# First cross-attention: one unit in four turned by TensorE, two score buffers, jobs moved off VectorE

## What is computed

```python
q = (x @ Wq + bq).reshape(1, B * N, H, hd);  kv = (cond @ Wkv + bkv)...
q = _fq_sym(q * scale, axis=-1); k = _fq_sym(k, axis=-1); v = _fq_sym(v, axis=2)
attn = softmax(einsum('bhqd,bhkd->bhqk', q, k), axis=-1)
attn = _fq_unsigned(attn, axis=-1)          # 0..255 steps of the row's largest value
out = einsum('bhqk,bhkd->bhqd', attn, v)
x = layernorm(x + out @ Wp + bp)
```

## Time and profile before

| | us |
|---|---|
| median of three runs (3065.53 to 3074.6) | 3072.57 |
| profiled execution | 3072.58 |
| its span, first to last instruction | 3070.2 |
| the attention part, first to last pass of VectorE (985.18 to 1683.08) | 697.9 |

### The profile page before, as it was taken

One profiled execution on the slowest core, in us unless ns is written; L12 is line 12 of the kernel. 1 busy time (PEld: TensorE's weight loads), 2 busy tenths in 40 slices (PEclk: granted clock), 3 DMA queues, 4 the chain that ended last, 5 costly groups with the idle time before them and its releaser, 6 DMA issues. The chain is left out here.

```text
span 3070.2 us, 48513 instructions
## 1 busy us (share of the span) xinstructions
PE 2597.4 (85%) x16300; PEld 1616.7 (53%) x16470; DVE 1887.5 (61%) x3971; ACT 1498.4 (49%) x2696; POOL 449.3 (15%) x679
## 2 busy tenths in 40 slices
PE   4999999999975677767776797899868789999997
PEld 2777777777753233333333454555445545555554
DVE  5677777677757899999998112566546622323232
ACT  1555555555544688888887111566545511111110
POOL 1111111112110121222221000111122200000000
PEclk9999999999997788888877898999989989999999
DMA  4000000000001999999999000000022000000000
GB/s 178 1 1 0 0 0 0 0 0 0 0 25 34 198 198 196 198 195 197 197 198 198 24 0 23 1 0 0 0 72 76 18 1 1 0 0 0 0 0 27
DMA packets 566849, 173.12 MB, mean 56 GB/s; under 512 B 535445, under 2 KB 564945, under 8 KB 565713
## 3 DMA queue, kind: packets, MB, share of 16 engines
q1 hardware_dynamic: 562168, 163.91, 28.5%
q10 hardware_dynamic: 4568, 7.74, 0.7%
HBM read 35.29 MB, written 2.10 MB: 12 GB/s over the span
## 5 line engine op out<-in xcount | busy, mean ns | idle before, releaser
L1577 DVE TENSOR_SCALAR_CACHE_REDUCE x_row<-x_p_s,x_nsq 128x1024 f32<-128x1024 f32 x512 | 622.9, 1276 | 15.3 <-PE x_p_s L1395 15.3
L1457 ACT ACTIVATE x_ints<-x_row,x_nb 128x2048 uint16<-128x2048 f32 x256 | 511.6, 1999 | 111.2 <-DMA x_turned<-x_ints 70.2
L1395 PE MATMUL x_p_s<-x_kT,x_qz 128*128 128x512 bf16 x937 | 346.0, 457 | 163.9 <-DVE x_row L1577 151.4
L2384 DVE TENSOR_TENSOR f_h<-f_act_g,f_p_u 128x512 f32<-128x512 f32 (+1 forms) x132 | 90.7, 687 | 521.1 <-PE f_p_y L2277 451.3
L2327 ACT ACTIVATE f_act_g<-f_p_g 128x512 f32<-128x512 f32 (+1 forms) x132 | 78.4, 597 | 548.1 <-PE f_p_g L2262 548.1
L2262 PE MATMUL f_p_g<-f_xT,f_wg 128*128 128x512 f32 (+1 forms) x528 | 258.4, 613 | 16.8 <-ACT f_xT L2314 10.1
L2262 PE MATMUL f_p_u<-f_xT,f_wu 128*128 128x512 f32 (+1 forms) x528 | 252.4, 601 | 0.0
L2277 PE MATMUL f_p_y<-f_wd,f_h 128*128 128x256 f32 (+1 forms) x1056 | 247.5, 379 | 0.0
L2277 PEld LDWEIGHTS f_p_y<-f_wd,f_h 128*128 128x128 f32 (+1 forms) x1056 | 200.6, 190 | 77.2 <-issue 55.6
L1395 PEld LDWEIGHTS x_p_s<-x_kT,x_qz 128*128 128x128 bf16 x1024 | 72.5, 104 | 316.1 <-DVE x_row L1577 293.4
L1408 PEld LDWEIGHTS x_p_o<-x_vi,x_turned 128*128 128x128 f16 x4096 | 144.2, 100 | 144.4 <-DMA x_turned<-x_ints 80.1
(11 more groups left out here) (357 smaller groups left out, 4804.0 us busy)
## 6 DMA issues: line engine op xcount, KB each, us to landing
x_turned<-x_ints SPq DMA_TRANSPOSE x256, 4.8
f_wg<-in_L_ffn_w_dram SPq DMA_DIRECT2D x2, 1408.0 KB, 7.3
f_wu<-in_L_ffn_w_dram SPq DMA_DIRECT2D x2, 1408.0 KB, 7.1
f_wd<-in_L_ffn_w_dram SPq DMA_DIRECT2D x1, 2816.0 KB, 11.1
a_wq<-in_L_attn_Wq_dram SPq DMA_DIRECT2D x1, 2048.0 KB, 8.2
a_wk<-in_L_attn_Wlk_dram SPq DMA_DIRECT2D x1, 2048.0 KB, 17.4
a_wv<-in_L_attn_Wlv_dram ACTq DMA_DIRECT2D x1, 2048.0 KB, 17.9
a_wo<-in_L_attn_Wo_dram ACTq DMA_DIRECT2D x1, 2048.0 KB, 23.6
```

What stands on the lines that cost most here:

```text
L1395: mm = pe.matmul(p_s[n % SLOTS][:, c * BANK:(c + 1) * BANK], qz[b % 2][:, par, a, :], kT[:, a, at:at + BANK], start=True, stop=True)
L1457: act.activation(ints[k][:, :], rows[k][:, :, :].rearrange("p s n -> p (s n)"), ACT.Exp, bias=nb[:, k:k + 1], scale=-1.0, accum_out=esum[: ...
L1577: dve.tensor_scalar(rows[k][:, half, :], p_s[n % SLOTS][:, :], nsq[:, b % 2, h:h + 1], HIGHEST, ALU.mult, ALU.min, accum_out=(low if half ...
L2384: i = dve.tensor_tensor(h[n % 2][0:m, :], act_g[n % 2][0:m, :], p_u[n % 2][0:m, :], ALU.mult)
```

## The change

One unit in four (u % 4 = 3, BY_ARRAY) is no longer transposed by a DMA. TensorE transposes its 16 blocks of 128 x 128 with the identity into a new PSUM tile `p_t` (two banks), three units after the scores, behind that unit's values. ScalarE copies `p_t` to `turned` as 1024 32-bit integers, after the next unit's exponential. To make room, `p_s` has two buffers instead of three. The residual is added in PSUM by a matmul of the identity with x within `project_o`, ScalarE copies the sum to y (`result_up`), and `residual` leaves VectorE. `scale`, the negated scale and `variance` go to GpSimd. The jobs move by one or two units: `turn_reps` to 9, `turn_o` to 12, `project_o` to 14, ScalarE's copies to 7, 8, 10 and 13, `inverse` to j=5, `statistics` and `moments` to 15, GpSimd's last three to 15.

```diff
     HIGHEST = 3.0e38
-    ROWS_KEPT, SLOTS, LATE = 4, 3, 6
+    ROWS_KEPT, SLOTS, LATE = 4, 2, 6
+    BY_ARRAY = ROWS_KEPT - 1
     PER_TILE = 2 * PAIRS
...
         p_s = [ps(f"p_s{i}", [P, HALF]) for i in range(SLOTS)]
+        p_t = ps("p_t", [P, 4 * BANK], BF16)
         p_o, p_w = ps("p_o", [P, BANK]), ps("p_w", [P, BANK])
         s_made, half_up, nb_up, e_up, o_made = (sem(n) for n in ("s_made", "half_up", "nb_up", "e_up", "o_made"))
-        t_in = [sem(f"t_in{k}") for k in range(ROWS_KEPT)]
+        t_in = [sem(f"t_in{k}") for k in range(BY_ARRAY)]
+        t_made, t_read = sem("t_made"), sem("t_read")
         x_turned, xT_up, q_made, q_up, amax_up, scl_up, rec_up, nsq_up = (sem(n) for n in (
...
                 k = u % ROWS_KEPT
-                sp.wait_ge(e_up, u + 1)
-                after(sp, o_made, u - ROWS_KEPT + 1)
-                sp.dma_start(turned[k][:, :, :], ints[k][:, :], transpose=True).then_inc(t_in[k], 16)
+                if k != BY_ARRAY:
+                    sp.wait_ge(e_up, u + 1)
+                    after(sp, o_made, u - ROWS_KEPT + 1)
+                    sp.dma_start(turned[k][:, :, :], ints[k][:, :], transpose=True).then_inc(t_in[k], 16)
                 if u == PER_TILE:
...
                 pe.matmul(p_w[:, 0:H], core.ones[:, :], core.bias("L0_xattn_bp"), start=True, stop=False)
+                pe.matmul(p_w[:, 0:H], core.ident[:, :], core.x[:, b, :], start=False, stop=False)
                 for t in range(KT):
...
                     mm.then_inc(s_made, 1)
+            def turn(u):
+                pe.wait_ge(e_up, u + 1)
+                after(pe, t_read, u // ROWS_KEPT)
+                for c in range(B):
+                    mm = pe.transpose(p_t[:, c * P:(c + 1) * P], ints[BY_ARRAY][:, c * P:(c + 1) * P].bitcast(BF16), core.identb[:, :])
+                mm.then_inc(t_made, 1)
+
             def values(u):
...
                     after(pe, o_read, b)
-                pe.wait_ge(t_in[k], 16 * (u // ROWS_KEPT + 1))
+                if k == BY_ARRAY:
+                    pe.wait_ge(t_read, u // ROWS_KEPT + 1)
+                else:
+                    pe.wait_ge(t_in[k], 16 * (u // ROWS_KEPT + 1))
                 for c in range(B):
...
                     values(u - LATE)
-                jobs(u, {1: [(turn_x, 1)], 3: [(project_q, 1)], 8: [(turn_reps, 1)], 11: [(turn_o, -1)], 13: [(project_o, -1)]})
+                if 0 <= u - 3 < UNITS and (u - 3) % ROWS_KEPT == BY_ARRAY:
+                    turn(u - 3)
+                jobs(u, {1: [(turn_x, 1)], 3: [(project_q, 1)], 9: [(turn_reps, 1)], 12: [(turn_o, -1)], 14: [(project_o, -1)]})
         @block.scalar
...
                 act.copy(oT[:, :, :].rearrange("p t n -> p (t n)"), p_w[:, 0:H]).then_inc(oT_up, 1)
+            def result_up(b):
+                act.wait_ge(y_made, b + 1)
+                after(act, x_up, b)
+                act.copy(y[:, :], p_w[:, 0:H]).then_inc(y_up, 1)
+
             def exps(u):
...
                 act.wait_ge(nb_up, u + 1)
-                after(act, t_in[k], 16 * (u // ROWS_KEPT))
+                if k == BY_ARRAY:
+                    after(act, t_made, u // ROWS_KEPT)
+                else:
+                    after(act, t_in[k], 16 * (u // ROWS_KEPT))
                 act.activation(ints[k][:, :], rows[k][:, :, :].rearrange("p s n -> p (s n)"), ACT.Exp, bias=nb[:, k:k + 1], scale=-1.0,
                                accum_out=esum[:, b, h:h + 1]).then_inc(e_up, 1)
+
+            def take_turned(u):
+                act.wait_ge(t_made, u // ROWS_KEPT + 1)
+                after(act, o_made, u - ROWS_KEPT + 1)
+                act.copy(turned[BY_ARRAY][:, :, :].rearrange("p k n -> p (k n)").bitcast(I32), p_t[:, :].bitcast(I32)).then_inc(t_read, 1)
             x_turned_up(0)
...
                     exps(u)
-                jobs(u, {1: [(query_up, 1)], 6: [(reps_up(0), 1)], 7: [(reps_up(1), 1)], 9: [(o_turned_up, -1)]})
+                if 0 <= u - 1 < UNITS and (u - 1) % ROWS_KEPT == BY_ARRAY:
+                    take_turned(u - 1)
+                jobs(u, {1: [(query_up, 1)], 7: [(reps_up(0), 1)], 8: [(reps_up(1), 1)], 10: [(o_turned_up, -1)], 13: [(result_up, -1)]})
         @block.gpsimd
...
                 return ap.rearrange("p (h d) -> p h d", d=XD)
+            def scales(b):
+                pool.wait_ge(amax_up, b + 1)
+                after(pool, rec_up, b)
+                pool.tensor_scalar(scl[:, :], amax[:, :], 1.0 / QMAX, FLOOR, ALU.mult, ALU.max).then_inc(scl_up, 1)
+
+            def negated(b):
+                pool.wait_ge(scl_up, b + 1)
+                after(pool, half_up, 2 * PER_TILE * (b - 1))
+                pool.tensor_scalar(nsq[:, b % 2, :], scl[:, :], -1.0, None, ALU.mult).then_inc(nsq_up, 1)
+
             def integers(b):
...
                 pool.tensor_tensor(o[:, :], o_raw[:, :], svu[:, :], ALU.mult).then_inc(o_up, 1)
+            def variance(b):
+                pool.wait_ge(mean_up, b + 1)
+                pool.tensor_scalar(mv[:, 1:2], mv[:, 1:2], LN_EPS, None, ALU.add).then_inc(var_up, 1)
+
             def root(b):
...
                 pool.tensor_scalar(core.x[:, b, :], y[:, :], mv[:, 0:1], ln_r[:, 0:1], ALU.subtract, ALU.mult).then_inc(x_up, 1)
-            for piece in (integers, whole, copies):
+            for piece in (scales, negated, integers, whole, copies):
                 piece(0)
...
                     shift(u)
-                jobs(u, {4: [(integers, 1)], 5: [(scale_values, -1), (whole, 1)], 6: [(copies, 1)], 13: [(root, -1)], 14: [(norm, -1)]})
+                jobs(u, {3: [(scales, 1)], 4: [(negated, 1)], 5: [(scale_values, -1), (integers, 1)], 6: [(whole, 1)], 7: [(copies, 1)],
+                         15: [(variance, -1), (root, -1), (norm, -1)]})
         @block.vector
...
                 dve.tensor_reduce(amax[:, :], heads(q[:, :]), AX.X, ALU.max, apply_absolute_value=True).then_inc(amax_up, 1)
-
-            def scale(b):
-                dve.wait_ge(amax_up, b + 1)
-                dve.tensor_scalar(scl[:, :], amax[:, :], 1.0 / QMAX, FLOOR, ALU.mult, ALU.max).then_inc(scl_up, 1)
             def inverse(b):
...
                 dve.reciprocal(rec[:, :], scl[:, :]).then_inc(rec_up, 1)
-                dve.tensor_scalar(nsq[:, b % 2, :], scl[:, :], -1.0, None, ALU.mult).then_inc(nsq_up, 1)
             def denominators(b):
...
                 dve.tensor_tensor(heads(o_raw[:, :]), heads(p_o[:, 0:H]), bcast(rden[:, :], [P, XH, XD]), ALU.mult).then_inc(o_read, 1)
-            def residual(b):
-                dve.wait_ge(y_made, b + 1)
-                after(dve, x_up, b)
-                dve.tensor_tensor(y[:, :], p_w[:, 0:H], core.x[:, b, :], ALU.add).then_inc(y_up, 1)
-
             def statistics(b):
...
                 dve.bn_aggr(mv[:, :], stats[:, :]).then_inc(mean_up, 1)
-
-            def variance(b):
-                dve.wait_ge(mean_up, b + 1)
-                dve.tensor_scalar(mv[:, 1:2], mv[:, 1:2], LN_EPS, None, ALU.add).then_inc(var_up, 1)
             def pass_over(u, half):
...
                     dve.tensor_scalar(vi[:, j * whole:(j + 1) * whole, :], vraw[j], ROUND, ROUND, ALU.add, ALU.subtract).then_inc(v_up, 1)
-            for piece in (largest, scale, inverse):
+            for piece in (largest, inverse):
                 piece(0)
...
                     pass_over(u, 0)
-                jobs(u, {4: [(scale, 1), (denominators, -1)], 13: [(statistics, -1)], 14: [(variance, -1)]})
+                jobs(u, {4: [(denominators, -1)], 5: [(inverse, 1)], 15: [(statistics, -1)]})
                 if u < UNITS:
                     pass_over(u, 1)
-                jobs(u, {3: [(largest, 1)], 4: [(inverse, 1), (divided, -1)], 12: [(residual, -1)], 13: [(moments, -1)]})
+                jobs(u, {3: [(largest, 1)], 4: [(divided, -1)], 15: [(moments, -1)]})
                 if u == ROWS_KEPT - 1:
```

## The result

The changed kernel takes 3113.3 us (median of 4 runs, 3112.1 to 3115.6) against 3073.6 for the kernel before beside it: a ratio of 1.014, interval 1.0127 to 1.0153. It is 40 us slower by these medians, and 43 by the ratio. The forecast was 3122, slower. Its profiled execution took 3112.3 us.

A forecast was written before the change was run, and what follows sets the result against it. VectorE was taken as the bound; its walk through the attention part summed to 708 us, 10 more than 697.9. With 40 for the slow clock and -1 at the end, 3072.6 became 3122 us (3092 to 3150).

The forecast's parts named there:

- ScalarE's backlog: ScalarE's lateness, starting anew at unit 6's turn, done 2.1 us after VectorE began that unit, and carried to y.
- VectorE is the bound: Attention part of the old kernel: VectorE's 512 passes of 1.205 us, 617 us of 697.9, set the pace.
- a floor of 651 us: VectorE's time for the attention part without the new waits: 617 + 22.7 + 6.7 + 5.
- Transposes off the queue: DMA queue: 192 transposes take some 524 us, so it no longer binds and the waits for it go.
- Two buffers, `divided`: VectorE at `divided`, unit 4: with two score buffers it waits 1.18 us for the last values, 18 us over 15 tiles.
- A turn's stall: VectorE behind TensorE's turn units: 0.12 us each at full clock, 6 us in all; 1.8 each at half clock.
- The wait of `statistics`: VectorE at `statistics` waits 2.2 us a tile for ScalarE's y, 33 us over 15 tiles.
- The clock: TensorE in the attention part: a quarter at half clock, 2.5 us a tile, 40 us in all, bounds 0 and 80.
- The weights' load: Load of the feed-forward weights in the attention part: some 8 us with a full queue, 5 taken (0 to 8).
- The end of the part: End of the attention part: a transfer shorter and one matmul longer, -1 us.
- full clock: Rival: without DMA waits TensorE stays at clock 1.00 in the attention part; 3082 us (3072 to 3092), chance 0.20.
- The faster case: Rival: ScalarE's backlog never forms, `divided` and `statistics` don't wait, VectorE runs at its floor; 3026 us, chance 0.12.

The follow-up runs named there:

- e1_jobs: Changed kernel without turns and with three score buffers, all 256 units transposed by DMA, so only the jobs moved: 3073.3 us.
- e9_untransposed_three: As e1_jobs, three score buffers, but units with u % 4 = 3 transposed by nobody after the first, that part of the result left out: 3016.0 us.
- e4_one_block_turned: Changed kernel with TensorE turning 1 block of 16 in each turned unit but the first, ScalarE's copy whole: 3082.6 us.
- e10_untransposed_two: As e9_untransposed_three, but with two score buffers instead of three: 3061.6 us.
- e3_divided_later: Changed kernel with `divided` on VectorE behind the first pass of unit 5 instead of the second of unit 4: 3095.8 us.
- e2_jobs_two: As e1_jobs, without turns, but with two score buffers instead of three: 3072.7 us.
- e6_values_between: Changed kernel with TensorE's values between the two halves of scores instead of behind both: 3076.8 us.
- e8_between_phase: Changed kernel with the values between the halves of scores and u % 4 = 1 turned instead of 3: 3086.2 us.
- e7_phase_one: Changed kernel with u % 4 = 1 turned instead of 3: 3084.0 us.

## Why the prediction was right, point by point

The direction, the size (3122 against 3113) and the two main mechanisms, the wait at `divided` and ScalarE's backlog, held. That the size is so near is in part luck: the price of the clock was some 17 us too high, and waits of 9 us that the sum lacks (5.0 for the query, 3.7 behind `turn_x`) hid half of it. In the order of its steps:

- *VectorE is the bound.* Wrong for the kernel before. Busy for 652 of 698 us it looked so, but e1_jobs took away the wait at the residual and won nothing, and e9_untransposed_three relieved the queue and won 57 us. The queue was the bound. The forecast did not suffer from this: its sum for the part was a new walk along VectorE, from a floor of 651 us (648.6 measured), and not a difference from the old waits.
- *Transposes off the queue.* Right: the DMA share fell to 0.77 (0.85 was named) and ScalarE's wait for it to 3.0 us.
- *Two buffers, `divided`.* 1.18 us forecast, 1.15 measured, in 15 tiles. Right.
- *A turn's stall.* 0.12 forecast at full clock. Behind unit 10, at full clock, the next pass started 0.1 us late in the changed kernel; unit 6 met the slow clock (1.5 to 1.7 us in most tiles; 1.8 was forecast for that case). The waits for scores came behind units 6 and 14, 45 of 60 us, and hardly behind 2 and 10, which the prediction had named with them.
- *The wait of `statistics`.* 2.2 us forecast, with unit 14 inside it. Measured 1.43 + 0.86 = 2.3, of which the profile gives the larger share to TensorE. Right in sum; the profile splits it between two rows. That ScalarE's backlog fixes the sum is seen in e4_one_block_turned, where TensorE's unit 14 is short: 0.67 + 1.71 = 2.4.
- *Not seen:* `largest` waits for the query, 14 times, 5.0 us in all, from the same backlog on ScalarE. I had followed the backlog to y alone.
- *The clock.* A quarter of the part at half clock, forecast; the mean of 0.89 is 22%. Its price of 40 us was too high: the slow clock at unit 6 cost 23 us, and the other long steps of the changed kernel ran mostly at 1.00. A share times a mean price was the wrong form: the slow clock sat at the same place of a tile again and again, and the price is that of what stands there.
- *The weights' load.* 5 us forecast; the tile it falls into lasts 48.8 us where its neighbours last some 46. Of the 8 us that the prediction reads off for the kernel before, 1.1 fall in later tiles.
- *The end of the part.* -1 forecast; from the last pass to the copy of the next stage it is 18.3 us (1724.70 to 1743.05) against 19.5.

Of the rivals, full clock did not come (0.89). The faster case names the point from which it decides, 2.9 us a tile, and the waits stayed above it (87 us by the rows above without the start and the end, 5.4 a tile). What it describes exists: with three buffers, which leave no room for `p_t`, e9_untransposed_three runs at the floor, 3016 us against the rival's 3026.

In the runs the mean clock of the part rose with the blocks that TensorE turned: 0.86 with none (e10_untransposed_two), 0.86 with one in sixteen (e4_one_block_turned), 0.89 with all. By the Trainium skill, "TensorE: Matmul & The Clock Gate", Part 4, transposes don't count as busy the way matmuls do, and the clock would have fallen with them. This case's runs do not bear it out.

With the queue relieved and no turn the clock rose as well, from 0.81 in e1_jobs to 0.86 in e9_untransposed_three, while TensorE's waits for transposes fell from 88.1 to 11.5 us; and still more than a fifth of the part ran at half clock, there and in the changed kernel. The section "HAM oscillation" of the same page of the Trainium skill has the clock fall in waits for DMA. That is borne out in part: such waits are not the only thing that goes with a low clock here.

## What to carry to other kernels

When two limits lie within a few per cent of each other, busy shares don't tell which one paces. Take away one wait and see whether the time moves: here 37.6 us of waiting were removed without a gain, and a buffer was given up without a loss, until the queue was relieved; then that same buffer was worth 46 us. So price the parts of such a change in the state in which they will run together, not one by one from the old kernel. And when work is added to an engine that feeds the pacing engine through two buffers, ask first where in its order it stands: moving the values by one half of the scores gave back 32 of the part's 42 us with no work removed. And where an edit is to explain a few us of a whole program, look whether they arose in the stage that was edited.

## What the runs showed of the hardware

- Sixteen bf16 transposes of 128 x 128 took TensorE 1.05 us at a clock of 1.00 and 1.87 at 0.50, and with nothing else changed VectorE's unit around them 2.51 and 4.20 us (e3_divided_later); the copy of the result as 128 x 1024 32-bit integers took ScalarE 1.01 us, no more than the bf16 copy of the earlier trace rows.
- A full queue moved one transpose of 512 KB in 699.1 / 256 = 2.73 us, at 195 GB/s, in three kernels with different waits around it (699.1 us in e1_jobs, 700.6 in e2_jobs_two, 697.9 in the kernel before).
- The slow clock met the turn of the same unit in tile after tile (unit 6 in the changed kernel, 15 of 16 tiles, and in e6_values_between, 14 of 16; units 0 and 8 in e8_between_phase, 13 each). Moving the turns to other units moved it or, in e7_phase_one, took it off most of them. What fixes its place was not settled; the idle time at `divided` was excluded by e3_divided_later.
